# First attention of a decoder layer, unrolled over its units and grouped by key head

## The reference

```python
# NH = 16 query heads, NKV = 4 key heads, QPG = 4 query heads for each key head, D = 128
qkv = jnp.einsum('bsh,ph->bsp', layernorm(x), weight_qkv).reshape(b, s, NKV, (QPG + 2) * D)
scores = jnp.einsum('bsgqd,btgd->bgqst', q, k) / sqrt(D)       # q, k, v are cut from qkv
scores = jnp.where(causal, scores, finfo.min)
out = jnp.einsum('bgqst,btgd->bsgqd', softmax(scores), v)
x = x + jnp.einsum('bse,he->bsh', out, weight_proj)
```

## Time and profile before

| | |
|---|---|
| time, median of 3 runs | 1064.57 us (1064.21 to 1069.08) |
| time of the profiled execution | 1061.68 us |
| its span | 1059.8 us |
| self-attention, first scores to last addition to x | 30.8 to 500.0 us |
| cross-attention and feed-forward | 500.3 to 1059.8 us |
| busy, whole span | PE 898.9, DVE 563.2, ACT 435.0, POOL 260.3 us |
| mean granted PE clock | 0.94 of 2.4 GHz |

### The profile page before, as it was taken

How to read it: one execution, slowest core, us unless ns; L and a number is a source line. 1 busy time by engine, 2 the same in 40 slices (tenths; PEclk the granted TensorE clock), 3 DMA queues, 4 the chain that set the end, 5 groups by cost and what they waited for, 6 DMA issues and landing times. The chain is left out here.

```text
span 1059.8 us, 17723 instructions
## 1 busy us (share of the span) xinstructions
PE 898.9 (85%) x5670; PEld 775.7 (73%) x5671; DVE 563.2 (53%) x1593; ACT 435.0 (41%) x1102; POOL 260.3 (25%) x448
## 2 busy tenths in 40 slices
PE   4799988999899999997878979796661799999990
PEld 3699977998799988997758567583631588888880
DVE  5755645565465655565484746556379223333225
ACT  4465635655466545663343323243061222222220
POOL 0233202322133212322011110101121344444430
PEclk9899999999999999999898989899875799999995
DMA  9100000000000000000160240707094111111117
GB/s 349 60 2 1 2 4 2 1 2 1 4 2 1 2 1 2 2 1 21 60 141 19 65 93 0 158 0 158 21 377 158 30 54 50 54 49 49 49 42 245
DMA packets 45596, 61.85 MB, mean 58 GB/s; under 512 B 3472, under 2 KB 36368, under 8 KB 45392
## 3 DMA queue, kind: packets, MB, share of 16 engines
q1 hardware_dynamic: 39664, 48.58, 15.9%
q0 software_dynamic: 3744, 10.23, 3.1%
q10 hardware_dynamic: 2112, 2.10, 0.6%
HBM read 34.81 MB, written 9.31 MB: 42 GB/s over the span
## 5 line engine op out<-in xcount | busy, mean ns | idle before, releaser
L246 POOL TENSOR_TENSOR prob<-prob,rinv 128x128 f32<-128x128 f32 (+1 forms) x256 | 124.5, 508 | 329.6 <-DVE rinv L312 329.6
L286 ACT ACTIVATE prob<-masked,negmax 128x128 f32<-128x128 f32 (+1 forms) x256 | 114.6, 448 | 182.4 <-DVE negmax L375 182.4
L301 DVE TENSOR_TENSOR pT_lo<-bank_t,pT_hi 128x384 fp32r<-128x384 f32 x128 | 70.7, 553 | 60.3 <-ACT pT_hi L258 60.3
L301 DVE TENSOR_TENSOR qT_lo<-bank_q,qT_hi 128x512 fp32r<-128x512 f32 x64 | 44.2, 691 | 94.4 <-ACT qT_hi L258 94.4
L38 PE MATMUL bank_s<-kT_hi,qT_hi 128*128 128x128 f32 (+1 forms) x256 | 78.1, 305 | 10.5 <-DVE WprojT_lo L332 6.5
L1444 DVE TENSOR_TENSOR f_xT_lo<-bank_o,f_xT_hi 128x256 fp32r<-128x256 f32 x39 | 16.6, 425 | 128.2 <-ACT f_xT_hi L1291 128.2
L375 DVE CUSTOM_DVE_ANT_0 masked<-bank_s,causal 128x128 f32<-128x128 f32 (+1 forms) x256 | 79.0, 346 | 0.0
L38 PE MATMUL bank_o<-pT_hi,v_hi 128*128 128x256 f32 (+1 forms) x256 | 74.9, 293 | 0.5 <-DVE pT_lo L301 0.5
L1589 PE MATMUL bank_y<-f_Wo,f_interT 128*128 x312 | 73.9, 380 | 0.8 <-ACT f_interT L1286 0.8
L38 PE MATMUL bank_y<-WprojT_hi,oT_hi 128*128 128x256 f32 x256 | 72.3, 282 | 0.0
L39 PE MATMUL bank_y<-WprojT_lo,oT_hi 128*128 128x256 f32 x256 | 71.9, 281 | 0.0
(11 more groups left out here) (276 smaller groups left out, 2518.8 us busy)
## 6 DMA issues: line engine op xcount, KB each, us to landing
b_VW_hi<-b_VWs_hi SPq DMA_DIRECT2D x32, 256.0 KB, 4.7
b_VW_lo<-b_VWs_lo SPq DMA_DIRECT2D x32, 256.0 KB, 4.8
f_W_lo<-in_L_ffn_w_kernel_dram SPq DMA_DIRECT2D x16, 512.0 KB, 9.7
f_Wo<-in_L_ffn_wo_kernel_dram SPq DMA_DIRECT2D x8, 512.0 KB, 9.3
stage<-n_L_attn_weight_qkv_dram SPq DMA_DIRECT2D x6, 512.0 KB, 7.7
stage<-_L_attn_weight_proj_dram SPq DMA_DIRECT2D x4, 512.0 KB, 10.8
WqT<-in_L_xattn_Wq_dram SPq DMA_DIRECT2D x1, 2048.0 KB, 20.0
b_wo<-in_L_xattn_Wo_dram SPq DMA_DIRECT2D x1, 2048.0 KB, 8.8
```

What stands on the lines that cost most here:

```text
L246: pool.tensor_tensor(prob[:, u % 3, a:b], prob[:, u % 3, a:b], rinv[:, u % 4, i:i + 1].to_broadcast([P, b - a]), ALU.mult)\
L286: act.activation(prob[:, s % 3, a:b], masked[:, s % 2, a:b], ACT.Exp, scale=-1.0, bias=negmax[:, s % 4, i:i + 1], accum_out=rowsum[:, s % ...
L301: dve.tensor_tensor(dst.lo, src, dst.hi.bitcast(F32), ALU.subtract).then_inc(free[n], 1)
```

## The change

The two hardware loops over pairs are gone: every engine walks over one list of 128 units and 8 more steps, written out. A pair's units are now ordered by key head, then sequence, then the four query heads of the key head.

- **Values.** The four pT of a group lie side by side, and a value product is made for all four at once, at every fourth step (`values`, s = 6, 10, ...): three matmuls of 512 columns into o0 (queries 0 to 127 of the sequence) and six into o1 (queries 128 to 255), in place of 24 matmuls of 256 and 128 columns. oT is copied out twice for a group.
- **Projection.** One head of one sequence for each step (`project`, six matmuls), after the transposes; the fourth of a group comes before the fill and the values of its step.
- **Fills.** One fill for a step at most, all into bank q, in 24 of a pair's 32 steps, and the transposes of xn in step 26. Steps 11, 13, 16, 18, 19, 21 and 24 have none. The next pair's xn, keys and queries are filled in steps 26 to 31, so there is no stretch without scores. The last pair has no next one: its steps 26 to 31 have no fills.
- **Order on DVE and PE.** DVE's copy of pT of unit s - 3 now stands in step s behind the mask of unit s.
- **Additions to x** are at steps 3 and 7 of the following pair.
- **Start.** PE waits for three of the ten weight pieces before the first scores. The other seven are split inside steps 0, 1, 3, 6, 8, 10 and 12 of the first pair. The transposes of xn use banks q and t. The statistics of a pair are taken during the pair before (steps 11 to 21), with POOL's power after step 17.
- **Memory and loads.** The buffer of four staged pieces is that of cross-attention's WqT, and xn is in the buffer of wk. So WqT, the context and its mask are loaded after all splits, wk after the last transposes of xn, and Wv at the start of cross-attention, ahead of Wo.

```diff
-            with eng.Fori(0, PAIRS - 1) as p:
-                for name, _ in body:
-                    run(p, name)
...
+        within = {0: ("v", 0), 2: ("v", 1), 3: ("v", 2), 5: ("v", 3), 8: ("k", 2), 10: ("k", 3)}
+        ahead = {-6: ("xt", 0), -5: ("k", 0), -4: ("q", 0, 0), -3: ("k", 1), -2: ("q", 0, 1), -1: ("q", 0, 2),
+                 1: ("q", 0, 3)}
+        for g in range(1, NKV):
+            for i, at in enumerate((-4, -2, -1, 1)):
+                within[8 * g + at] = ("q", g, i)
+        split_at = {0: "q1", 1: "p0", 3: "q2", 6: "p1", 8: "q3", 10: "p2", 12: "p3"}
+        def pv_at(s):
+            return (s - 6) // QPG if s >= 6 and (s - 6) % QPG == 0 and (s - 6) // QPG < ALL // QPG else None
+        def t_at(s):
+            return s - 2 if 0 <= s - 2 < ALL else None
...
@@ ACT, step s
+                    if s >= 1 and t_at(s - 1) is not None:
+                        high(("t", t_at(s - 1)))
+                    if s < ALL:
+                        act.wait_ge(masked_ready, 2 * (s + 1))
...
@@ DVE, step s
+                    if 1 <= s <= ALL:
+                        invert(s - 1)
+                    if s < ALL:
+                        n = banks.bank(("s", s))
+                        dve.wait_ge(full[n], banks.count(("s", s)))
...
+                    if s >= 1 and t_at(s - 1) is not None:
+                        low(("t", t_at(s - 1)))
+                    if r == 3 and p >= 1:
+                        residual(p - 1, 0)
+                    if r == 7 and p >= 1:
+                        residual(p - 1, 1)
+                    if fill_at(s):
+                        low(fill_at(s))
+                    if pv_at(s) is not None:
+                        low(("o", pv_at(s), 0))
+                        low(("o", pv_at(s), 1))
+                    if s in split_at:
+                        split_lo(split_at[s])
...
@@ PE
+                def transposes(u):
+                    pe.wait_ge(prob_ready, 2 * (u + 1))
+                    wait_free(("t", u))
...
+                def values(G):
+                    copied(("t", G * QPG + QPG - 1))
...
+                    mm3(pe, bank["o0"][:], vg[:, 2 * b, :], pT[:, 0, :, :].view("p h q -> p (h q)"), True, True)
+                    mm3(pe, bank["o1"][:], vg[:, 2 * b, :], pT[:, 1, :, :].view("p h q -> p (h q)"), True, False)
+                    mm3(pe, bank["o1"][:], vg[:, 2 * b + 1, :], pT[:, 2, :, :].view("p h q -> p (h q)"), False, True)
...
@@ PE, step s
+                        scores(s)
+                    proj_now = proj_at(s)
+                    if proj_now and proj_now[1] == QPG - 1:
+                        project(*proj_now)
...
+                        fill(name)
+                    if pv_at(s) is not None:
+                        values(pv_at(s))
+                    if t_at(s) is not None:
+                        transposes(t_at(s))
+                    if proj_now and proj_now[1] < QPG - 1:
+                        project(*proj_now)
+                    if late_fill_at(s):
+                        fill(late_fill_at(s))
...
@@ SP
+                sp.wait_ge(w_lo, len(PIECES))
                 cm.load_cross_inputs(sp)
+                sp.wait_ge(full["q"], banks.count(last))
+                cm.load_cross_keys(sp)
...
+                sp.dma_start(wv[:], Wv).then_inc(wv_loaded, 16)
                 sp.dma_start(wo[:], Wo.rearrange("(h p) n -> p h n", p=P)).then_inc(wo_loaded, 16)
```

More of the change, by code:

```diff
@@ L151, in self_attention @@
[L151 to L187, removed]
@@ L260, in split_hi @@
[L260 to L283, removed]
-                        act.wait_ge(masked_ready, p * 2 * UNITS + 2 * (s + 1))
+                    src = bank[n][:, 0:width]
@@ new lines, in high, with split_hi @@
+                    if len(dst.hi.shape) == 3:
+                        src = src.rearrange("p (a b) -> p a b", a=dst.hi.shape[1])
+                    act.wait_ge(full[n], banks.count(name))
+                    act.activation(dst.hi, src, ACT.Copy).then_inc(half[n], 1)
+                def split_hi(n):
+                    act.wait_ge(w_loaded[n], 16)
+                    act.activation(part[n].hi, staged[n], ACT.Copy).then_inc(w_hi, 1)
+                split_hi("k")
+                high(first[0][0])
@@ new lines, in _ @@
+                high(first[1][0])
+                split_hi("q0")
+                high(first[2][0])
+                high(first[3][0])
+                split_hi("v")
+                for name, _ in first[4:]:
+                    high(name)
+                for s in range(STEPS):
+                    if s >= 1 and t_at(s - 1) is not None:
+                        high(("t", t_at(s - 1)))
+                    if s < ALL:
+                        act.wait_ge(masked_ready, 2 * (s + 1))
+                        if s >= 3:
+                            act.wait_ge(full["t"], banks.count(("t", s - 3)))
@@ L350, in _ @@
[L350 to L371 removed]
+                split_lo("k")
@@ L404, in fill, with copied @@
-                def fill(p, name):
-                    what, i = name
-                    n = uses.bank_of(p, name)
-                    wait_free(p, name)
+                    before = banks.uses[n][count - 2]
+                    if before[0] == "s":
+                        pe.wait_ge(masked_ready, 2 * (before[1] + 1))
+                    else:
+                        pe.wait_ge(free[n], count - 1)
+                def copied(name):
+                    n, count = banks.at[name]
+                    pe.wait_ge(free[n], count)
@@ L420, in fill, with scores @@
                     ins.then_inc(full[n], 1)
-                def wait_copied(p, name):
-                    pe.wait_ge(free[uses.bank_of(p, name)], uses.count_freed(p, name))
+                def scores(u):
+                    p, g, b, i = unit(u)
+                    n = banks.bank(("s", u))
+                    wait_free(("s", u))
+                    if b == 0:
+                        copied(("q", p, g, i))
+                        if i == 0:
+                            copied(("k", p, g))
+                    mm3(pe, bank[n][:, 0:P], qT[:, i, b * S:b * S + P], kT[:, g, b * S:b * S + P], True, True)
+                    mm3(pe, bank[n][:, P:CW], qT[:, i, b * S + P:b * S + S], kT[:, g, b * S:b * S + S],
+                        True, True).then_inc(full[n], 1)
@@ new lines, in project @@
+                def project(G, i):
+                    p, g, b, _ = unit(G * QPG)
+                    y = bank[("y0", "y1")[b]]
+                    if i == 0:
+                        copied(("o", G, 0))
+                        copied(("o", G, 1))
+                        if g == 0 and p > 0:
+                            pe.wait_ge(x_updated[b], p)
+                    h = QPG * g + i
+                    for t in range(2):
+                        ins = mm3(pe, y[:, t * HID:(t + 1) * HID], oT[:, i, t, :], WprojT[:, h, :],
+                                  h == 0 and t == 0, h == NH - 1)
+                    if h == NH - 1:
+                        ins.then_inc(y_full[b], 1)
```

447 lines of the change are left out of this document (230 added, 217 removed).

## The result

| | before | changed |
|---|---|---|
| median | 1065.21 us (4 runs) | 1091.07 us (4 runs, 1088.09 to 1092.83) |
| span of the profiled execution | 1059.8 us | 1089.5 us |
| first scores | 30.84 us | 21.38 us |
| self-attention ends | 500.0 us | 530.1 us |
| mean granted clock | 0.940 | 0.937 |

The ratio is 1.023, with a 95% interval of 1.020 to 1.027: the kernel became slower, by 26 us. I had forecast 12 to 13 and a range of 1057 to 1100. The side is right, the size is about half.

A forecast was written before the change was run, and what follows sets the result against it. PE was taken to bound self-attention. With pairs of 118.0 us, self-attention ends 10.7 us later; plus 2 for the clock, 12.7 on 1061.68 gives 1074.4, stated as 1077 us against the median; range 1057 to 1100.

The forecast's parts named there:

- the 3.08 us of a step: Self-attention step without values: scores 0.69, wait for transposes 1.41, transposes 0.27, projection 0.71, with or without a fill.
- work of a pair falls to 103.2: PE's work in a self-attention pair falls from 111.3 to 103.2 us; grouped values save 0.81 x 32 = 26.
- The scores always follow a projection: On PE, scores follow a projection or another 256- or 512-column matmul, saving 0.05 x 128 = 6 us.
- 0.10 to PE: Handover from the end of DVE's copy of pT to PE's transposes, taken as 0.10 us within the 1.41.
- I take 2 us: Allowance for PE's clock falling because of short idles in self-attention: 2 us, between nothing and 32 to 40 in all.
- About 1.3: Added to a pair for statistics and normalizations at DVE's step ends and keys waiting for the late xn copy: 1.3 us.
- The wait inside each step: PE's transposes wait for DVE's copy of pT, 1.41 us after the scores; some 50 such waits, 60 us in total.
- A fill covers it: In steps with a fill, its 1.38 us on PE covers the wait for pT; the step is 3.08 us.
- Values after the mask's delay: In the step after values, the next mask starts at 5.67 against 5.30 by the scores, so 3.08 + 0.37 = 3.45 us.
- PE at its pace: Rival: the copy of pT is early enough, a pair takes its 103.2 us of work, about 1015 us; chance 0.15.
- the ring of DVE and ACT: Mask, exp, fill copies, reciprocal and handovers on DVE and ACT in steps with a fill: 2.9 us, so no reserve.
- The clock rival: Rival: many short PE idles make the clock swing, 20 to 38 us more, 1097 to 1115 us; chance 0.13.

The follow-up runs named there:

- experiment 2: Changed kernel with PE's projection of a step ahead of the transposes instead of behind them: 1060.31 us, ratio to the kernel before 0.9965.
- experiment 3: Changed kernel with POOL multiplying only 16 columns of each block, leaving out most of the softmax's normalization: 1088.26 us.
- experiment 5: Kernel before the change, with only DVE's copy of pT held back until behind the next step's mask: 1090.03 us, ratio 1.023.
- experiment 1: Changed kernel with DVE's copy of pT moved ahead of the mask: 1076.07 us, ratio to the kernel before 1.011.
- experiment 7: Changed kernel with projection first, all splits in front, and DVE copying o's second half behind the next mask where that step has a fill: 1058.61 us.
- experiment 4: Changed kernel with all seven weight splits back ahead of the steps, none inside them: 1085.95 us.
- experiment 8: Changed kernel with each value product of 512 columns cut into two of 256: 1090.20 us.
- experiment 9: Changed kernel with each value product of 512 columns cut into four of 128: 1150.75 us.
- experiment 6: Changed kernel with the projection ahead of the transposes and all weight splits ahead of the first scores: 1057.91 us, ratio to the kernel before 0.992.

## Why the prediction was right in its side and wrong in its size

The steps that failed are sizes in the sum: the 3.08 us of a step, which is 3.20 (two terms of it, 0.71 for the projection and 0.10 to PE), and the 2 us for the clock, which are 7.

- **"PE paces it"; "work of a pair falls to 103.2"**: the work fell less. Term by term, the value product of one unit, 0.72 us, held 0.08 us which does not belong to the values: the first matmul behind the transposes, 428.20 to 428.40 instead of 0.12. The change moves that to the projection, which takes 0.78 us and not 0.71. The saving of a group is not 0.81 but 0.81 - 4 x 0.07 = 0.53 us: 17 us in all and not 26. About 6 of these 9 us count in the time: 0.07 in each of some 85 steps behind the first fourteen whose projection follows the transposes.
- **"The scores always follow a projection"** is not so either: behind a step with values they follow the transposes, and take 0.77 us (195.14 to 195.91). This cost nothing, since the mask was later still.
- **"0.10 to PE"**: it is 0.15 in all 49 waits for this copy. In the kernel before it was 0.06 in six of eight such waits and 0.15 in two, and I took a number in between; what sets it isn't known. In 85 steps this is 4 us. With both terms the step is 3.20 instead of 3.08, 2.8 us a pair over its steps with and without values.
- **"I take 2 us" for the clock**: it cost about 7. It fell behind waits of 1.9 us in step 19 of the first three pairs (1.5 us each), at step 14 of the first (1.6), and at the end (0.8).
- **"About 1.3"** for statistics, normalizations and the keys' wait: measured against a plain step of their kind, and with the clock's part taken off, steps 15, 19, 26 and 27 take 1.5 us more. This term was right.
- **Start**: first scores 0.5 us earlier than said (21.4 and 0.7 to issue them, forecast 22.6). Steps 0 to 13 take 59.6 us instead of 57.2. **End**: 15.5 us from the issue of the last scores instead of 13.9, half of it the clock.
- The sum: self-attention ends at 530.1 instead of 510.7, 19.4 us: 1.9 to step 14, 4.9 in the rest of the first pair (3.0 of it the clock), 4.6 in each of the next two (1.5 of it the clock), 1.8 in the last, 1.6 behind it (0.8 of it the clock). By cause this is 7 us for the clock, where I had set aside 2 for the whole kernel, and 10 for the two terms of the step.
- **The wait inside each step** was right, and experiments 2, 3 and 5 show it: PE waits 51 us for the copy of pT (I had said 60), an order that covers it gives 31 us back (5 of them the clock), and this order alone in the old kernel costs 23 us. **"A fill covers it"** was the weak sentence: 1.38 us doesn't cover 1.46, and experiment 5 shows what a tenth or two of a microsecond is worth when it is repeated in every step.
- **Values after the mask's delay**: 3.55 - 3.20 = 0.35, forecast 0.37.
- **The rivals**: PE at its pace didn't happen, and in experiment 1 moving that one copy doesn't bring it: the ring of DVE and ACT is next. The clock rival, 20 to 38 us, came in a small form, about 7 us. The rule of the Trainium skill on many short idles (TensorE: Matmul & The Clock Gate, section A second HAM failure mode) is borne out to that extent: self-attention has seven stretches at 1.2 GHz in 510 us, where the kernel before had three. The middle pairs have 0.99 all the same, and the first has 0.95, where it had 0.97. Its 131 ns for 512 columns (section Back-to-back issue gap) isn't seen: 199.39 to 200.54 in the changed kernel is 0.23 us for each again. Loads and code cost nothing that can be seen: behind self-attention the span is 559.4 us, before 559.8.
- **Open**: a middle pair with the projection first takes 115.4 us against some 106 of PE work. Which order brings that down, beyond the trade of experiment 7, wasn't tried. Nor was the last pair's share by itself: its steps without fills could hold the start of cross-attention.

## What to carry to other kernels

Before a step of an in-order pipeline is rewritten, follow one unit through the queues and ask of each wait of the bounding engine whether what releases it can run before this step's own work. A copy that moves behind a wait of its own engine puts the whole chain into every step, and hundredths of a microsecond count as often as the step is repeated. When a saving is taken from the distance between two starts, check that the cost goes away with the instructions: a first matmul that is dear because of what is ahead of it stays with whoever comes next. And before a few microseconds are put down to an edit, lay the granted clock of both traces side by side: here one stretch at half clock is worth 1.5 us, and it moved with the waits.

## What the runs showed of the hardware

- The first matmul (128 x 128 by 256 columns) behind the three float32 transposes takes 0.20 to 0.21 us until the next starts, the following ones 0.11 to 0.12, with a wait ahead of the transposes or without. It stays with whoever comes: the first matmul of scores (128 columns) takes 0.15 behind the transposes (449.06 to 449.21 in experiment 2) and 0.06 behind a projection (198.70 to 198.76 in the changed kernel).
- At the full granted clock a matmul with its own weights, in a run of its like, costs 0.11 us for 128 columns, 0.118 for 256 and 0.23 for 512. Cutting products of 512 into 256 changed nothing (1090.20 against 1091.07 us); cutting into 128 cost 60 us.
- The granted clock is 0.99 in the middle pairs, where PE waits 1.3 to 1.9 us in one step of five. Behind the wait of 1.9 us in step 19 it fell to 1.2 GHz in 10 of 15 cases (the first three pairs of the changed kernel and of experiments 3, 4, 8 and 9), for about 1.5 us of time each. In experiments 1, 2, 6 and 7, where that wait is 0.5 to 1.3 us, it fell there in none of 12.
- Self-attention is over when DVE's last addition ends; its last row is this, 29 us behind its counterpart in the earlier trace rows:

```profile
529.38 0.69 DVE L386 TENSOR_TENSOR x_all<-bank_y,x_all 128x512 f32<-128x512 f32 x1 [2.57 <-PE bank_y L40]
```
